# A two-norm, two-convolution kernel: another order of norms and results, and result c folded into its last product and copied by ScalarE

## Chip, cores and metric

The kernel runs on one core of one Trainium2 chip. The metric is the device time of one execution in microseconds. Shown are the median of several runs, and one profiled execution with its trace.

## The reference, cut to what matters

`x` is (16, 384, 32, 32) in fp32, `offset` is (48, 2). All arithmetic is fp32.

```python
x = x + _L0_conv_ref(_gn(x), L0_conv_offset)
x = x + _L1_conv_ref(_gn(x))
return x
```

`_gn` is a group norm with 32 groups of 12 channels per image. `_L0_conv_ref` shifts each block of 8 channels by its own whole number of pixels, zeroes what comes from outside, and applies one 3x3 Gaussian kernel per block, depthwise. Only a few of the 48 blocks have an offset that leaves anything in view. `_L1_conv_ref` multiplies the 384 channels of each pixel, padded to 512, by a Hadamard matrix over the square root of 512 and keeps the first 384 outputs.

## The kernel before

**Data and quarters.** The 16 images go in four quarters of four. A ring of ten places in SBUF holds whole images: 384 channels are three tiles a, b, c of 128 partitions, 1024 pixels each. SP loads them (L389), also stores the results from the same place (L421), and a place is loaded again once its three stores have landed.

**First norm and convolution.** For each quarter, statistics of every channel are taken, on ScalarE by two passes over a tile (`take_stats`, L559) and on VectorE by `bn_stats` (L1044); `dve_tiles` (L51) says which engine takes which tile. VectorE turns them into means (`means`, L1059), PE sums them over groups (`sum_means`, L687), VectorE spreads them (L1074), PE sums again (`sum_about`, L696), and `unit_moments`, ScalarE's `root_first` and `unit_scales` give the scale of each block. Nine blocks in view are computed in three units of a quarter: two of four blocks each ("strips"), and one of one block cut in four bands. SP fetches a unit's rows twice from DRAM, shifted and plain (`fetch`, L394). ScalarE norms the shifted rows (`centre`, L576), PE transposes them (`transposes`, L715), VectorE masks them (L1118), PE convolves (L746), and VectorE adds the plain rows and takes statistics of the sum (`add`, L1130). GpSimd then writes the sum x1 to DRAM (`leave`, L477) and gathers its rows back over the images in the ring with six indirect DMAs per quarter (`gather`, L496). Other channels have x1 = x and stay. `more_blocks` handles offsets with more blocks in view and does not run here.

**Second norm.** `all_moments`, `sum_second` (PE, L777), `second_shift`, ScalarE's `root_second` and `second_scale` give the scale of each channel and image, and `sum_bias` with `second_bias` the output bias.

**Products and results.** Per image n, PE accumulates into one pair of PSUM banks, `ps[n % 2]`. `product_a` (L798) multiplies tile a in fp32 by a scaled 128x128 Hadamard block; `product_b` subtracts tile b, given as two fp16 parts that ScalarE (`high`, L612) and VectorE (`low`, L1262) make; `product_c` adds tile c in fp32. That is the result for output tile b. VectorE's `result` (L1268) adds bias and x1 and writes it over the ring. Then `add_b` adds twice tile b: output tile a. Then `add_c` subtracts twice tile c: output tile c. Each waits for the result before it, since it overwrites the same banks, and `product_a` of image n waits for all three results of image n-2. The order is b, a, c. The weight of tile c lies in `w_c` in two versions, one scaled by h and one by -2h, made by ScalarE for the first image of a quarter (`weights_c`, L607) and by GpSimd for the others (L505).

**Order.** Every engine's order is written out by hand. The head does quarter 0 up to its products. Then window w (w = 0 to 3) holds the results of images 4w to 4w+3 and, among them, norm, units and second norm of quarter w+1 and the statistics of quarter w+2; `j` is the image's number in its quarter. SP's loop is at L459, GpSimd's at L544, ScalarE's at L643, PE's at L874, VectorE's follows its head. Three places matter below: VectorE does `means(q)` ahead of the first result of a window; it does all of mask, add and `all_moments` at j = 1 ahead of the first result of j = 2; and PE's second sums wait for these moments:

```python
if j == 1:
    ...
    if units:
        mask(g + 2)
        add(g + 1)
        add(g + 2)
        all_moments(q)
if j == 2:
    result(n, 1)
```

## Time and profile before

| | us |
|---|---|
| median of 3 runs (289.92 to 291.0) | 290.21 |
| profiled execution, its own time | 289.43 |
| its span in the trace | 287.6 |
| DVE busy | 178.9 |
| PE busy | 177.8 |
| ACT busy | 117.4 |
| POOL busy | 72.4 |

The span runs from the first to the last instruction of the profiled execution; 1.8 us of its time lie outside. PE is TensorE, DVE VectorE, ACT ScalarE, POOL GpSimd, SP the engine that issues most DMAs. A row of a timeline gives the start and the duration of an instruction or of several merged ones, and in brackets the idle time of its engine before it with what released it. L815 is the matmul of tile b, L825 that of tile c, L808 that of tile a, L1272 the result, L1265 the low part, L618 the high part, L565 and L568 ScalarE's two statistics passes.

### The profile page before, as it was taken

The numbers are of one execution on the slowest core, as the hardware profiler recorded it, in microseconds if no ns is written. First come the engines' busy times: TensorE is split into PE (matmuls) and PEld (weight loads), VectorE is DVE, ScalarE is ACT, GpSimd is POOL, SyncE is SP. The second block draws the span as 40 slices with busy tenths as digits, with TensorE's granted clock in tenths as the row PEclk, the third lists the DMA queues.
The fourth block names the chain that finished last, engine by engine and source line by source line (L and its number), as shares of the span: only waits on it lengthen the run. The fifth ranks groups of instructions, "written<-read, shape, count | busy, mean of one in ns | idle before, by whom it ended". The sixth has DMA issues, their size and how long they took to land.

```text
span 287.6 us, 3917 instructions
## 1 busy us (share of the span) xinstructions
PE 177.8 (62%) x1228; PEld 89.7 (31%) x1228; DVE 178.9 (62%) x411; ACT 117.4 (41%) x179; POOL 72.4 (25%) x101
## 2 busy tenths in 40 slices
PE   1300158306529776586597981957779839899962
PEld 1200046203204524242245351412345424233420
DVE  2779745921757585745976638448966476666642
ACT  0295088013937595098038780692231001311000
POOL 0197001328600000581200004742000036720000
PEclk9999999955969999599869997799799977999998
DMA  6999999915555176399899983896874325855544
GB/s 212 400 416 407 239 289 408 411 63 162 154 172 223 75 215 263 132 312 351 279 258 320 377 293 149 267 359 234 214 274 172 147 93 170 291 217 219 219 194 170
DMA packets 23626, 70.65 MB, mean 246 GB/s; under 512 B 5952, under 2 KB 6976, under 8 KB 23024
## 3 DMA queue, kind: packets, MB, share of 16 engines
q1 hardware_dynamic: 18480, 60.90, 60.4%
q0 software_dynamic: 5120, 9.45, 10.5%
q8 instruction: 11, 0.18, 0.2%
q14 instruction: 15, 0.12, 0.1%
HBM read 60.89 MB, written 29.88 MB: 316 GB/s over the span
## 4 chain that ended last, share of the span: by engine, by line
PE 39%; DVE 35%; ACT 10%; issue 8%; DMA 4%; POOL 1%; DVEq 0%; SPq 0%; POOLq 0%; ACTq 0%
PE ps L825 12%; DVE ring L1272 10%; PE ps L815 8%; PE ps L730 7%; PE ps L808 6%; DVE halves L1049 5%; ACT junk L565 4%; DVE unit_half L1140 4%; DVE plain L1137 4%; ACT junk L568 4%; PE ps L711 4%; DMA ring<-x_rows,index 2%; DVE flip L1109 2%; DMA x_rows<-plain 2%; DVE parts L1265 1%
## 5 line engine op out<-in xcount | busy, mean ns | idle before, releaser
L1272 DVE SCALAR_TENSOR_TENSOR ring<-ps,out_bias,ring 128x1024 f32<-128x1024 f32 x48 | 61.5, 1282 | 36.7 <-PE ps L825 20.3
L825 PE MATMUL ps<-ring,w_c 128*128 128x512 f32 x128 | 61.0, 615 | 5.7 <-DVE ring L1272 5.6
L815 PE MATMUL ps<-parts,had_sb 128*128 128x512 f16 x128 | 41.0, 463 | 13.8 <-DVE ring L1272 9.7
L618 ACT ACTIVATE parts<-ring,scale 128x1024 f16<-128x1024 f32 x16 | 18.0, 1143 | 62.7 <-PE ps L815 50.0
L808 PE MATMUL ps<-ring,w_a 128*128 128x512 f32 x64 | 32.0, 624 | 12.8 <-DMA ring<-x_rows,index 8.5
L565 ACT ACTIVATE junk<-ring 128x1024 f32<-128x1024 f32 x32 | 36.6, 1144 | 4.0 <-DMA ring<-x_pad 2.0
L481 POOL DMA_DIRECT2D x_rows<-plain x8 | 5.0, 620 | 128.7 <-DVE plain L1137 128.7
L568 ACT ACTIVATE junk<-ring 128x1024 f32<-128x1024 f32 x32 | 36.8, 1149 | 1.0
L825 PEld LDWEIGHTS ps<-ring,w_c 128*128 128x128 f32 x128 | 23.8, 197 | 35.2 <-issue 21.7
L1265 DVE SCALAR_TENSOR_TENSOR parts<-ring,scale,parts 128x1024 f16<-128x1024 f32 x16 | 20.6, 1288 | 18.9 <-ACT parts L618 18.9
L491 POOL DMA_INDIRECT ring<-x_rows,index x24 | 24.4, 1019 | 18.6 <-issue 18.6
L815 PEld LDWEIGHTS ps<-parts,had_sb 128*128 128x128 f16 x128 | 12.5, 112 | 37.5 <-DVE ring L1272 15.1
L730 PE MATMUL ps<-conv_w,flip 128*32 128x192 f32 (+2 forms) x640 | 23.4, 304 | 1.1 <-DVE plain L1137 1.1
L692 PE MATMUL ps<-means,sum_w 128*128 128x12 bf16 x28 | 1.3, 171 | 34.0 <-DVE means L1042 34.0
L808 PEld LDWEIGHTS ps<-ring,w_a 128*128 128x128 f32 x64 | 11.7, 198 | 28.8 <-issue 28.1
L1049 DVE BATCH_NORM_STATS2 halves<-ring 128x6 f32<-128x512 f32 x32 | 19.6, 673 | 1.4 <-issue 1.4
L730 PEld LDWEIGHTS ps<-conv_w,flip 128*32 128x32 f32 x640 | 17.9, 116 | 5.7 <-issue 2.6
L598 ACT ACTIVATE root<-var,geo_sb 128x12 f32<-128x12 f32 x4 | 1.2, 304 | 43.8 <-DVE var L1245 43.8
L1137 DVE TENSOR_TENSOR plain<-ps,plain 128x1024 f32<-128x1024 f32 (+1 forms) x12 | 11.3, 938 | 9.9 <-PE ps L730 9.9
L711 PE MATMUL ps<-geo_sb,shifted 128*128 128x128 f32 x72 | 11.8, 308 | 8.6 <-DVE flip L1109 5.9
L1109 DVE TENSOR_TENSOR flip<-ps,view 128x1024 f32<-128x1024 f32 x8 | 9.8, 1225 | 10.0 <-PE ps L711 9.8
L580 ACT ACTIVATE shifted<-shifted,unit_norm 128x1024 f32<-128x1024 f32 (+1 forms) x12 | 11.6, 1019 | 6.5 <-DMA shifted<-x_pad 3.7
(151 smaller groups left out, 168.6 us busy)
## 6 DMA issues: line engine op xcount, KB each, us to landing
ring<-x_pad SPq DMA_DIRECT2D x16, 1536.0 KB, 12.2
out<-ring SPq DMA_DIRECT2D x48, 512.0 KB, 3.4
shifted<-x_pad SPq DMA_DIRECT2D x32, 128.0 KB, 5.0
plain<-x_pad SPq DMA_DIRECT2D x32, 128.0 KB, 3.8
x_rows<-plain POOLq DMA_DIRECT2D x8, 512.0 KB, 4.8
shifted<-x_pad SPq DMA_DIRECT2D x16, 32.0 KB, 4.4
plain<-x_pad SPq DMA_DIRECT2D x16, 32.0 KB, 3.0
x_rows<-plain POOLq DMA_DIRECT2D x16, 32.0 KB, 1.7
```

The lines of the kernel that those rows point to most:

```text
L491: pool.indirect_dma_start(ring[:, t, first_place:first_place + 2, :].rearrange("p b n -> p (b n)"), None, x1_rows[q][0:BIND * slots, :].re ...
L565: act.activation(junk[:, :], image, ACT.Identity, bias=image[:, 0:1], scale=-1.0, accum_out=accum[:, q % 2, 0, t, b:b + 1]).then_inc(act_s ...
L568: act.activation(junk[:, :], image, ACT.Square, bias=image[:, 0:1], scale=-1.0, accum_out=accum[:, q % 2, 1, t, b:b + 1]).then_inc(act_sta ...
L711: last = pe.transpose(turned[:, j // 4, 128 * (j % 4):128 * (j % 4) + rows], shifted[0:rows, u, 128 * j:128 * (j + 1)], eye[0:rows, 0:rows])
L730: last = pe.matmul(summed[32 * s:32 * s + 32, bank, 32 * (lo - 16 * bank):32 * (hi - 16 * bank)], pixels[:, j, 32 * s:32 * s + 32], conv_w ...
L808: pe.matmul(ps[n % 2][:, h, :], w_a[:, n % 4, :], ring[:, 0, place_of(n), 512 * h:512 * (h + 1)], start=True, stop=False, skip_group_check ...
L815: last = pe.matmul(ps[n % 2][:, h, :], had_sb[:, 128 * sign:128 * (sign + 1)], parts[:, n % 2, part, s, 512 * h:512 * (h + 1)], start=Fals ...
L825: last = pe.matmul(ps[n % 2][:, h, :], w_c[:, n % 4, twice, :], ring[:, 2, place_of(n), 512 * h:512 * (h + 1)], start=False, stop=True, sk ...
L1049: last = dve.bn_stats(halves[:, q % 2, t, b, h, :], ring[:, t, place_of(i), 512 * h:512 * (h + 1)])
L1137: dve.tensor_tensor(plain[:, u, 0:width], sums, plain[:, u, 0:width], ALU.add).then_inc(x1_ready, 1)
L1265: dve.scalar_tensor_tensor(parts[:, n % 2, 1, s, :], ring[:, 1 + s, place_of(n), :], scale[:, q % 2, 1 + s, b:b + 1], parts[:, n % 2, 0, s ...
L1272: dve.scalar_tensor_tensor(ring[:, t, place_of(n), :], pixels_of(ps[n % 2]), out_bias[:, q % 2, t, b:b + 1], ring[:, t, place_of(n), :], A ...
```

## The change

Norm 1 is moved ahead of the results: VectorE's `means(1)`, `spread_means(1)`, `unit_moments(1)` and `unit_scales(1)`, PE's two sums and ScalarE's root now stand in the head, and the statistics of quarter 1 with them, split six tiles to six. SP fetches the shifted rows of two units of quarter 1 before it waits for the gathered rows, loads before it stores, and does the next window's wait and shifted fetch at j = 2. The results of a window are interleaved with masks and adds, the second sums stand ahead of the last image's additions, and all products of the next quarter's first image follow them. Result c loses its VectorE instruction: `fold_weights` builds -2h times the scale plus the identity per image, so that `add_c` adds x1 of tile c in the same matmuls, and ScalarE's `result_c` copies PSUM with the bias to the ring. `result_done` now counts two per image, `result_c_done` the third.

In the diff the orders of ScalarE, PE and VectorE are shown as they are after it, without the removed lines, which are in the code above.

```diff
 def dve_tiles(i):
     if i < 2 * QUARTER:
-        return ((0, 1), (0,))[i // QUARTER]
+        return (0, 1) if i < QUARTER + 2 else (0,)
     return (0, 1) if i % QUARTER == QUARTER - 1 else ()
...
-        w_c = sb("w_c", [128, 4, 2, 128])
+        w_c = sb("w_c", [128, 4, 128])
+        w_fold = sb("w_fold", [128, 2, QUARTER, 128])
...
-            def fetch(q):
+            def fetch(q, which, units=range(UNITS)):
                 def rows(tile, u, s, which):
                     if SLOTS_OF[u] == 1:
                         return tile[32 * s:32 * s + 32, u, 0:WIDTH_OF[u]], x_bands(q, at[PER_UNIT * u][which])[:, s, :]
                     return tile[32 * s:32 * s + 32, u, :], x_slot(q, at[PER_UNIT * u + s][which])
 
-                for u in range(UNITS):
-                    if q:
-                        sp.wait_ge(flipped, UNITS * (q - 1) + u + 1)
-                    for s in range(PER_UNIT):
-                        home, source = rows(shifted, u, s, 1)
-                        sp.dma_start(home, source).then_inc(shifted_in[u], 16)
-                for u in range(UNITS):
-                    if q:
+                for u in units:
+                    if which == 1:
+                        if q:
+                            sp.wait_ge(flipped, UNITS * (q - 1) + u + 1)
+                    elif q:
                         sp.wait_ge(x1_out[u], left(u, q - 1))
                         sp.wait_ge(x1_stat, UNITS * (q - 1) + u + 1)
                     for s in range(PER_UNIT):
-                        home, source = rows(plain, u, s, 0)
-                        sp.dma_start(home, source).then_inc(plain_in[u], 16)
+                        home, source = rows((plain, shifted)[which], u, s, which)
+                        sp.dma_start(home, source).then_inc((plain_in, shifted_in)[which][u], 16)
...
             def store(n, t):
-                sp.wait_ge(result_done, CT * n + ORDER.index(t) + 1)
+                if t == 2:
+                    sp.wait_ge(result_c_done, n + 1)
+                else:
+                    sp.wait_ge(result_done, 2 * n + ORDER.index(t) + 1)
                 sp.dma_start(out_v[n][:, t, :], ring[:, t, place_of(n), :]).then_inc(store_out[place_of(n)], 16)
...
-            fetch(0)
+            fetch(0, 1)
+            fetch(0, 0)
             for i in range(QUARTER + 2, RING):
                 sp.wait_ge(load_in[place_of(i - 4)], 16)
                 load(i)
             active = sp.value_load(count_i[0:1, 0:1], min_val=0, max_val=OFFSETS)
+            fetch(1, 1, (0, 1))
             more_blocks(0)
             rows_back(0)
-            fetch(1)
+            fetch(1, 1, (2,))
+            fetch(1, 0)
             for n in range(BATCH):
                 w, j = n // QUARTER, n % QUARTER
-                store(n, 1)
-                store(n, 0)
                 if n >= 1 and n - 1 + RING < BATCH:
                     load(n - 1 + RING)
-                store(n, 2)
+                for t in ORDER:
+                    store(n, t)
                 if j == 1 and w + 1 < QUARTERS:
                     more_blocks(w + 1)
+                if j == 2 and w + 2 < QUARTERS:
+                    rows_back(w + 1)
+                    fetch(w + 2, 1)
                 if j == 3 and w + 2 < QUARTERS:
-                    rows_back(w + 1)
-                    fetch(w + 2)
+                    fetch(w + 2, 0)
...
-                pool.tensor_scalar(w_c[:, n % 4, 0, :], geo_of("h"), scale[:, q % 2, 2, b:b + 1], None, ALU.mult)
-                pool.tensor_scalar(w_c[:, n % 4, 1, :], geo_of("h"), scale[:, q % 2, 2, b:b + 1], -2.0, ALU.mult, ALU.mult)
+                pool.tensor_scalar(w_c[:, n % 4, :], geo_of("h"), scale[:, q % 2, 2, b:b + 1], None, ALU.mult)
                 pool.tensor_scalar(w_a[:, n % 4, :], geo_of("h"), scale[:, q % 2, 0, b:b + 1], None, ALU.mult).then_inc(weights_ready, 1)
...
-                act.activation(w_c[:, n % 4, 0, :], geo_of("h"), ACT.Copy, scale=scale[:, q % 2, 2, 0:1])
-                act.activation(w_c[:, n % 4, 1, :], geo_of("minus_2h"), ACT.Copy, scale=scale[:, q % 2, 2, 0:1]).then_inc(first_weights_c, 1)
+                act.activation(w_c[:, n % 4, :], geo_of("h"), ACT.Copy, scale=scale[:, q % 2, 2, 0:1]).then_inc(first_weights_c, 1)
+
+            def result_c(n):
+
+
+                q, b = n // QUARTER, n % QUARTER
+                act.wait_ge(product_done, CT * n + CT)
+                act.activation(ring[:, 2, place_of(n), :], pixels_of(ps[n % 2]), ACT.Identity,
+                               bias=out_bias[:, q % 2, 2, b:b + 1]).then_inc(result_c_done, 1)
...
-            for i in range(QUARTER, QUARTER + 2):
+            for i in range(QUARTER, 2 * QUARTER):
                 for t in act_tiles(i):
                     take_stats(i, t)
             root_second(0)
             weights(0)
             weights_c(0)
-            for n in range(2):
-                high(n, 0)
-            for i in range(QUARTER + 2, 2 * QUARTER):
-                for t in act_tiles(i):
-                    take_stats(i, t)
-            for n in range(BATCH):
-                w, j = n // QUARTER, n % QUARTER
+            high(0, 0)
+            high(1, 0)
+            root_first(1)
...
+            for w in range(QUARTERS):
+                n, g = QUARTER * w, UNITS * (w + 1)
                 units, stats_next = w + 1 < QUARTERS, w + 2 < QUARTERS
                 ahead = QUARTER * (w + 2)
+                high(n + 2, 0)
+                result_c(n)
+                if units:
+                    if w:
                         root_first(w + 1)
+                    for u in range(UNITS):
+                        centre(g + u)
+                if stats_next:
+                    take_stats(ahead, 0)
+                high(n + 3, 0)
+                if stats_next:
+                    take_stats(ahead, 1)
+                result_c(n + 1)
+                if stats_next:
+                    take_stats(ahead, 2)
+                    take_stats(ahead + 1, 0)
+                result_c(n + 2)
+                if stats_next:
+                    take_stats(ahead + 1, 1)
+                if units:
+                    more_blocks(w + 1)
+                    root_second(w + 1)
+                    weights(n + QUARTER)
+                    weights_c(n + QUARTER)
+                if stats_next:
+                    take_stats(ahead + 1, 2)
+                result_c(n + 3)
+                if stats_next:
+                    take_stats(ahead + 2, 0)
+                if units:
+                    high(n + QUARTER, 0)
+                    high(n + QUARTER + 1, 0)
+                if stats_next:
+                    take_stats(ahead + 2, 1)
+                    take_stats(ahead + 2, 2)
+                    take_stats(ahead + 3, 2)
 
...
-                    pe.wait_ge(result_done, CT * (n - 1))
+                    pe.wait_ge(result_done, 2 * (n - 1))
+                    pe.wait_ge(result_c_done, n - 1)
...
+                weight = w_fold[:, q % 2, b, :] if twice else w_c[:, n % 4, :]
                 for h in range(2):
-                    last = pe.matmul(ps[n % 2][:, h, :], w_c[:, n % 4, twice, :], ring[:, 2, place_of(n), 512 * h:512 * (h + 1)],
+                    last = pe.matmul(ps[n % 2][:, h, :], weight, ring[:, 2, place_of(n), 512 * h:512 * (h + 1)],
                                      start=False, stop=True, skip_group_check=True)
...
-                pe.wait_ge(result_done, CT * n + 1)
+                pe.wait_ge(result_done, 2 * n + 1)
                 product(n, 0, B_TWICE, True).then_inc(product_done, 1)
 
             def add_c(n):
-                pe.wait_ge(result_done, CT * n + 2)
+                pe.wait_ge(result_done, 2 * n + 2)
+                pe.wait_ge(fold_ready, n // QUARTER + 1)
                 tile_c(n, 1).then_inc(product_done, 1)
...
             sum_second(0)
+            sum_means(1)
             product_a(0)
+            sum_about(1)
             sum_bias(0)
             product_b(0)
             product_c(0)
             product_a(1)
...
+            for w in range(QUARTERS):
+                n, g = QUARTER * w, UNITS * (w + 1)
+                units = w + 1 < QUARTERS
+                add_b(n)
+                product_b(n + 1)
+                if units and w:
+                    sum_means(w + 1)
+                add_c(n)
+                if units and w:
+                    sum_about(w + 1)
+                product_c(n + 1)
+                product_a(n + 2)
+                if units:
+                    transposes(g)
+                add_b(n + 1)
+                product_b(n + 2)
+                if units:
+                    transposes(g + 1)
+                    convolve(g)
+                add_c(n + 1)
+                product_c(n + 2)
+                if units:
+                    transposes(g + 2)
+                    convolve(g + 1)
+                product_a(n + 3)
+                add_b(n + 2)
+                product_b(n + 3)
+                if units:
+                    convolve(g + 2)
+                add_c(n + 2)
+                product_c(n + 3)
+                if units:
+                    more_blocks(w + 1)
+                    sum_second(w + 1)
+                add_b(n + 3)
+                if units:
+                    sum_bias(w + 1)
+                add_c(n + 3)
+                if units:
+                    product_a(n + 4)
+                    product_b(n + 4)
+                    product_c(n + 4)
+                    product_a(n + 5)
...
-                if q >= 2:
-                    link(mean_and_variance(QUARTER * q + QUARTER - 1, stats_at[QUARTER * q + QUARTER - 1]))
+                if q:
+                    for i in range(QUARTER * q, QUARTER * q + QUARTER):
+                        if dve_tiles(i):
+                            last = mean_and_variance(i, stats_at[i])
+                    link(last)
...
+            def fold_weights(q):
+                for b in range(QUARTER):
+                    last = dve.scalar_tensor_tensor(w_fold[:, q % 2, b, :], geo_of("minus_2h"), scale[:, q % 2, 2, b:b + 1], geo_of("eye"),
+                                                    ALU.mult, ALU.add)
+                last.then_inc(fold_ready, 1)
...
             mask(0)
+            take_stats(4, (0,))
             mask(1)
+            stats_at[4] = take_stats(4, (1,))
+            take_stats(5, (0,))
             add(0)
             mask(2)
-            stats_at[4] = take_stats(4)
+            stats_at[5] = take_stats(5, (1,))
             add(1)
-            mean_and_variance(4, stats_at[4])
             add(2)
             all_moments(0)
             second_shift(0)
             second_scale(0)
+            fold_weights(0)
+            stats_at[6] = take_stats(6)
+            stats_at[7] = take_stats(7)
+            means(1)
+            spread_means(1)
             low(0, 0)
+            unit_moments(1)
+            low(1, 0)
             bias_at[0] = second_bias(0)
-            low(1, 0)
-            for i in range(QUARTER + 1, 2 * QUARTER):
-                stats_at[i] = take_stats(i)
-                if i > QUARTER + 1:
-                    mean_and_variance(i - 1, stats_at[i - 1])
-            link(mean_and_variance(2 * QUARTER - 1, stats_at[2 * QUARTER - 1]))
-            for n in range(BATCH):
-                w, j = n // QUARTER, n % QUARTER
-                q = w + 1
-                units, stats_next, g = q < QUARTERS, w + 2 < QUARTERS, UNITS * (w + 1)
+            unit_scales(1)
...
+            for w in range(QUARTERS):
+                n, g, q = QUARTER * w, UNITS * (w + 1), w + 1
+                units, stats_next = q < QUARTERS, w + 2 < QUARTERS
                 ahead = QUARTER * (w + 2)
+                result(n, 1)
+                if units and w:
+                    means(q)
+                result(n, 0)
+                if units and w:
+                    spread_means(q)
+                if units and w:
+                    unit_moments(q)
+                low(n + 2, 0)
+                if units and w:
+                    unit_scales(q)
+                result(n + 1, 1)
+                if units:
+                    keep_moments(q)
+                    mask(g)
+                result(n + 1, 0)
+                if units:
+                    mask(g + 1)
+                    add(g)
+                low(n + 3, 0)
+                if units:
+                    mask(g + 2)
+                result(n + 2, 1)
+                if units:
+                    add(g + 1)
+                result(n + 2, 0)
+                if units:
+                    add(g + 2)
+                    all_moments(q)
+                if units:
+                    second_shift(q)
+                result(n + 3, 1)
+                if units:
+                    second_scale(q)
+                result(n + 3, 0)
+                if units:
+                    bias_at[q] = second_bias(q)
+                    fold_weights(q)
+                if stats_next:
+                    stats_at[ahead + 3] = take_stats(ahead + 3)
+                if units:
+                    low(n + 4, 0)
+                    low(n + 5, 0)
```

## Rows read from the trace of the kernel before

**Rows 1.** The page: busy time of each engine; GB/s moved in 40 equal slices

```profile
PE 177.8 (62%) x1228; PEld 89.7 (31%) x1228; DVE 178.9 (62%) x411; ACT 117.4 (41%) x179; POOL 72.4 (25%) x101
...
GB/s 212 400 416 407 239 289 408 411 63 162 154 172 223 75 215 263 132 312 351 279 258 320 377 293 149 267 359 234 214 274 172 147 93 170 291 217 219 219 194 170
```

**Rows 2.** Stretches: length, busy of PE, PEld, DVE, ACT, POOL, then clock, DMA share, GB/s

```profile
83.30:141.90 58.60, 42.65 (x304) 20.69 (x304) 38.67 (x83) 33.32 (x52) 13.92 (x21) 0.91 0.65 224
141.90:202.20 60.30, 44.38 (x304) 21.60 (x304) 38.69 (x84) 33.43 (x52) 13.94 (x21) 0.89 0.86 284
202.20:254.50 52.30, 40.93 (x301) 20.65 (x302) 34.92 (x68) 9.05 (x12) 14.89 (x21) 0.90 0.58 193
254.50:287.60 33.10, 24.42 (x68) 9.40 (x66) 17.93 (x14) 2.30 (x2) 0.00 (x0) 0.97 0.51 206
```

**Rows 3.** Waits: engine, line, releaser: us in total, times, longest

```profile
PE ps L692 <- DVE means L1042: 34.0, 4, 22.3
...
PE ps L782 <- DVE scrap L942: 20.4, 4, 5.4
```

**Rows 4.** Timeline of DVE: start us, us, operation, [idle before it, releaser]

```profile
81.87 0.17 DVE L1062 TENSOR_SCALAR deviation<-accum 128x8 f32<-128x8 f32 x1 [4.61 <-ACT junk L568]
...
101.60 1.21 DVE L1137 TENSOR_TENSOR plain<-ps,plain 128x1024 f32<-128x1024 f32 x1
...
104.29 1.23 DVE L1265 SCALAR_TENSOR_TENSOR parts<-ring,scale,parts 128x1024 f16<-128x1024 f32 x1
...
114.46 0.38 DVE L1137 TENSOR_TENSOR plain<-ps,plain 128x256 f32<-128x256 f32 x1
...
117.57 1.28 DVE L1272 SCALAR_TENSOR_TENSOR ring<-ps,out_bias,ring 128x1024 f32<-128x1024 f32 x1
```

**Rows 5.** Timeline of PE, head and window 0

```profile
67.20 3.58 PE L808 MATMUL ps<-ring,w_a 128*128 128x512 f32 x4 [8.50 <-DMA ring<-x_rows,index]
...
72.56 1.88 PE L825 MATMUL ps<-ring,w_c 128*128 128x512 f32 x4
...
84.65 1.89 PE L815 MATMUL ps<-parts,had_sb 128*128 128x512 f16 x4 [0.77 <-DVE ring L1272]
...
93.17 1.04 PE L711 MATMUL ps<-geo_sb,shifted 128*128 128x128 f32 x8
...
96.67 2.72 PE L730 MATMUL ps<-conv_w,flip 128*32 128x160 f32 x80
...
99.32 1.90 PE L815 MATMUL ps<-parts,had_sb 128*128 128x512 f16 x8
...
101.74 3.70 PE L825 MATMUL ps<-ring,w_c 128*128 128x512 f32 x8 [0.52 <-DVE ring L1272]
...
111.62 1.18 PE L739 MATMUL ps<-conv_w,band_flip 128*128 128x160 f32 x8
...
118.91 3.25 PE L815 MATMUL ps<-parts,had_sb 128*128 128x512 f16 x8 [0.62 <-DVE ring L1272]
```

**Rows 6.** Timeline of ACT

```profile
39.45 1.15 ACT L565 ACTIVATE junk<-ring 128x1024 f32<-128x1024 f32 x1 [0.19 <-issue]
...
42.05 1.15 ACT L565 ACTIVATE junk<-ring 128x1024 f32<-128x1024 f32 x1
...
59.61 0.30 ACT L598 ACTIVATE root<-var,geo_sb 128x12 f32<-128x12 f32 x1 [9.82 <-DVE var L1245]
...
89.78 2.87 ACT L580 ACTIVATE shifted<-shifted,unit_norm 128x1024 f32<-128x1024 f32 x3 [1.18 <-DVE unit_norm L1103]
```

**Rows 7.** Timeline of POOL; then DMA issues at 49.1 and 136.3, to landing

```profile
62.69 1.10 POOL L491 DMA_INDIRECT ring<-x_rows,index  x1 [5.51 <-issue]
...
119.49 1.10 POOL L491 DMA_INDIRECT ring<-x_rows,index  x1 [2.35 <-issue]
...
x_rows<-plain POOLq DMA_DIRECT2D x1, 512.0 KB, 8.4
...
ring<-x_pad SPq DMA_DIRECT2D x1, 1536.0 KB, 10.5
```

138 lines of the change are left out of this document (5 added, 133 removed).

## The prediction

> **What bounds the kernel now.** I began with the page: the busiest engine, DVE, works 62% of the span and PE 62% [rows 1]. So no engine is full, and the time lies in how the engines wait for each other. The table by stretches [rows 2] is cut at the starts of the first result of batches 0, 4, 8 and 12. It leaves a head of 83.3 us before its first row, and gives three windows of 58.6, 60.3 and 52.3 us (four batches of results, the unit work of the next quarter beside them) and a tail of 33.1 us. In each window PE is busy 41 to 44 us and DVE 35 to 39 us; the tail has PE 24.4 of 33.1. The granted clock is 0.89 to 0.91 of full in the windows.
>
> The waits by releaser [rows 3] name the two holes on PE: 34.0 us before the sums of the means and 20.4 us in four waits of about 5 us before the second sums (L782). In the DVE timeline [rows 4] the head's hole is plain: DVE sits idle for 4.61 us at 81.87 for ScalarE's statistics, then computes the means, and only then takes result b of batch 0 at 83.3, though PE had that product from 74.4 on (the fp32 matmuls at 72.56 last 1.88) [rows 5]. Result b of batch 2 starts at 117.57 because VectorE's order puts it behind all the adds and moments; PE had finished it at about 105.4 (101.74 + 3.70) [rows 5]. So the order written by hand binds, not the amount of work.
>
> **The change, part by part.** Prices of one piece, at the full clock: four fp16 matmuls 0.87 (eight take 1.90), four fp32 ones 1.72, the eight transposes 1.0, a strip convolution 2.7, the band one 1.18 [rows 5]; on DVE a result or a low part 1.20 to the next start, an add with its statistics 2.7 (101.60 to 104.29) [rows 4]; on ACT a tile of statistics 2.6 (39.45 to 42.05), a high part, one pass over the same 128x1024, 1.15, the three centrings 2.87 [rows 6].
>
> *The head.* Norm 1 moves ahead of the results. ScalarE's share of its statistics goes from 8 tiles to 6, all before the second root: 6 x 2.6 = 15.6 from 39.45 ends at 55.1; the root came at 59.61 [rows 6], so this is hidden, with 4.5 to spare for loads that land late. VectorE takes 6 tiles at 1.2 instead of 4; four fit into its waits for transposes and convolutions, two (2.5 us), the four fold instructions (below) and the means (about 2.7 with the aggregates) stand between 60.7 and 67. Product a of batch 0 waits for its gathered rows until 67.20 [rows 5], so they are hidden too, with a few tenths to spare; bound: 0 to 1.5. The first result then starts when product c ends, 74.4, not 83.3: minus 8.9. Against this, SP now fetches the shifted rows of two units of quarter 1 (8 x 128 KB, 1 MB) at 40 to 45 us, behind the last ring loads. Beside those the x1 write of the first unit takes 8.4 us to land [rows 7], and the gather waits for all the x1 writes. At the 410 GB/s of that stretch [rows 1] 1 MB is 2.6 us: between 0 (the fetch only queues behind its own) and 2.6 I take 1.5. The page DMA: Bandwidth & Descriptors of the Trainium skill (Queues, rings and completion order) says each DMA engine goes round-robin between queues, packet by packet. By that rule the fetch would not stand ahead of the writes but only keep their share low for longer, which is inside the same bounds. **Start of the results: 74.4 + 1.5 = 75.9.**
>
> *ScalarE takes result c.* DVE loses 16 of 48 results (19 us at 1.20), ACT gets 16 copies out of PSUM. No row shows ACT reading PSUM; the nearest are the high part (1.15) and a centring of 1024 columns, an Identity with bias too, whose three take 2.87 with one of a quarter's size, so about 1.25: I take 1.15, and up to 1.3. The page VectorE: DVE Perf Modes (The TRN2 errata) gives a ScalarE copy from PSUM fewer fixed cycles than one from SBUF; its figures would make it about 1.0 us, an estimate, and the sum would be the same, since these copies end before product a of the next-but-one batch asks for them. What they cost is the place in ACT's queue, counted below. PE's work is equal: the identity is folded into a weight it loads anyway. The fold is four DVE instructions on 128x128 per quarter; bounds 0.17 (a vector of 128x8) and 0.38 (the band add, 128x256) each [rows 4], I take 0.9 for the four, behind PE's last product c, so nothing on the path. POOL and ACT lose one weight scaling each.
>
> *Window 0.* From the first result, PE's own order now has hardly a hole: product a 1.7; b twice 1.75 and a 0.5 wait for result a; c twice 3.5; a 1.7 (9.2); transposes (10.2); b twice (11.9); transposes and strips (15.6); c twice (19.05); band transposes, strips (22.1); a (23.8); b twice (25.55); bands (26.75); c twice (30.2); second sums (30.8). Masks, adds and results of DVE fit beside it: the first add ends at 18.4, before the second strips end; the second add's 2.7 and result a of batch 2 end at 26.1, before 26.75. Moments end at 29.9. What used to be 5 us before L782 is gone. Then comes the part bound by turns: second shift 0.9 and result b 1.25 (33.0), b again and its result a (35.3), c again (37.0). ACT then has result c (38.2), one tile of statistics (40.8) and the high part (42.0); DVE low part (43.3); half of product b and product c: **45.5**. The x1 round trip is near but not last: from the band add (114.46 [rows 4]) to the first gather (119.49) are 5.0, and 4.5 more to its landing (62.69 to 67.20, [rows 5, 7]), for which I take 5.2 beside stores, 1.4 later for tile b: 27.2 + 5.0 + 1.4 + 5.2 = 38.8.
>
> *Window 1.* Ten tiles (26 us) of statistics, four copies, four high parts and three centrings fill ACT for about 39 us. Behind the high parts (43.1) three tiles are still queued: 7.8, to 50.9, 5.4 into window 1. VectorE's means of that window wait for them and sit ahead of result a, so c again starts at 8.6 instead of 4.0, and with the sums the transposes end at 15.1, not 10.2: plus 4.9, **50.4**. This is a new wait, and the same one moves on into window 2, where no statistics follow: there the gather ends last: 32.1 + 5.0 + 1.4 + 5.2 = 43.7, then 1.15 + 1.25 + 0.45 + 1.75: **48.3**.
>
> SP: the wait for the gathered rows and 12 fetches of the next window now precede the stores of batch n+3 and load 12. Issued near 51 in window 0, landing 10.5 later as at 136.3 [rows 7], it comes at 61.5, just when ScalarE wants it (15.6 into window 1). Zero, at most 2 per window.
>
> *The clock.* After a hole PE runs at half speed for a while: four fp16 matmuls took 1.89 at 84.65 and eight 3.25 at 118.91, against 0.87 and 1.90 [rows 5], together 2.4 us a window. The holes are shorter in window 0 (about 4 us while the high part is made) and a real 4 us returns with the means: 1.5, 2.4 and 2.4.
>
> *The tail* keeps its order on PE; its last result is now ACT's, 1.15 for 1.28: 33.1.
>
> **Sum.** 75.9 + 47.0 + 52.8 + 50.7 + 33.1 = 259.5 against a span of 287.6. Around the span lay 1.8 (289.43 profiled): 261.3. The median of the runs is 0.8 above that execution: **262**.
>
> **The rivals.**
> *ScalarE's queue and the loads bind more than I say.* For it: ACT waits in strict order for a product, a load, a root and a product again, and load 12 has no slack. Each of windows 0 to 2 is 3 to 4 longer: 262 + 10 = 272. Chance 0.17.
> *Only the head gains.* If the windows keep their 58.6, 60.3 and 52.3 because the x1 round trip and the half clock hold them, the time is 290.2 - 7.4 (83.3 - 75.9) = 283. Against it: result b of batch 2 alone waited 12 us for nothing. Chance 0.08.
> *The copies do not help.* If an ACT copy out of PSUM took 2 us or more, the tail's product a would wait, since product a follows result c after only one more fp32 product, 1.72: 0.5 x 12 batches, some 6 us: 268. Chance 0.05.
> *Slower.* One mechanism: SP stands at the gathered rows while the ring places of stored batches wait for reloading; loads 12 to 15 arrive late, ACT's statistics wait in front of its copies, and so PE's product a. It decides once load 12 lands about 14 us later than needed in each of two windows, that is once the sum loses its 28. The landing of 10.5 us [rows 7] speaks against this. Chance 0.05: 0.04 for 293, 0.01 that it stops at no change.
> *Better than forecast.* The clock stays full and the fetch costs nothing: 256. Chance 0.12.
>
> **How the numbers follow.** The forecast itself has 0.53, with its own range of 258 to 267 (DMA 0 to 2.6, hidden head work 0 to 1.5, clock 0 to 7). The range 255 to 275 takes in the better case, the slow copy and the ScalarE rival, leaving out 283 and the slower one. A difference of 0.5% is about what a measurement of this kernel can tell from none. Faster 0.95, same 0.01, slower 0.04.
>
> **What would show it.** Right: first result at 75 to 77; PE's waits for means far below 34 us and for the second sums under 1 each; in windows 1 and 2 a DVE wait of 3 to 5 for ACT before the means; result c copies of 1.0 to 1.3; window lengths near 47, 53 and 51. Wrong: a gather that starts after 66; a product a released by an ACT copy; ACT idle for ring loads.

## The result, and the profile after

The changed kernel takes **267.25 us** (median of 4 runs, 266.63 to 267.69) against 290.16 (4 runs) for the kernel before: a ratio of **0.9204**, 95% interval 0.9174 to 0.9234. The forecast was 262, its range 255 to 275. The profiled execution took 266.63, with a span of 264.6, for which the sum said 259.5. A second set of runs, later and on another chip, gave 268.07 (0.9244, 0.9175 to 0.9313). All ratios leave out single executions that came out 1.5% or more above the fastest of their kernel, while the medians take in all, and two of the profiles below, of no prefetch and of light and stats, are of such an execution, 4.4 and 3.1 us above the median.

The page of the changed kernel, busy time of each engine and four groups of lines (busy and mean ns, then idle time before them):

```profile
PE 178.2 (67%) x1228; PEld 93.7 (35%) x1228; DVE 166.8 (63%) x417; ACT 127.3 (48%) x183; POOL 68.7 (26%) x89
...
L1298 DVE SCALAR_TENSOR_TENSOR ring<-ps,out_bias,ring 128x1024 f32<-128x1024 f32 x32 | 41.0, 1282 | 27.7 <-PE ps L841 18.3
L622 ACT ACTIVATE ring<-ps,out_bias 128x1024 f32<-128x1024 f32 x16 | 17.8, 1113 | 68.7 <-PE ps L841 68.7
...
L631 ACT ACTIVATE parts<-ring,scale 128x1024 f16<-128x1024 f32 x16 | 17.9, 1141 | 28.7 <-PE ps L830 14.9
```

PE works as long as before (178.2 for 177.8); what went is its waiting. VectorE has 32 results for 48 and ScalarE the other 16, at 1113 ns each. The stretches, cut where they were cut before (first result of batches 0, 4, 8, 12), and then three pieces of windows 0 and 1:

```profile
75.28:123.66 48.38, 41.83 (x289) 21.53 (x288) 31.59 (x59) 31.86 (x47) 13.97 (x19) 0.89 0.71 239
123.66:184.52 60.86, 46.75 (x305) 23.52 (x304) 35.03 (x82) 39.35 (x60) 13.91 (x20) 0.83 0.84 286
184.52:231.65 47.13, 41.74 (x305) 22.11 (x304) 32.76 (x78) 14.88 (x19) 13.55 (x18) 0.93 0.79 267
231.65:264.60 32.95, 24.41 (x68) 9.53 (x66) 12.80 (x10) 6.75 (x6) 0.00 (x0) 0.97 0.47 191
...
75.30:105.50 30.20, 29.68 (x261) 16.27 (x260) 21.47 (x37) 18.65 (x25) 3.95 (x8) 1.00 0.75 250
...
139.50:161.00 21.50, 21.38 (x239) 12.82 (x237) 16.18 (x31) 15.10 (x24) 3.19 (x6) 1.00 0.92 308
161.00:184.40 23.40, 13.62 (x27) 5.76 (x28) 9.86 (x21) 15.31 (x25) 9.63 (x12) 0.71 0.74 272
```

Against [rows 2]: the head lost 8.0 us, window 0 10.2 and window 2 5.2. **Window 1 lost nothing** (60.9 for 60.3). It holds a stretch of 21.5 us in which PE does not stop at all, at full clock, and behind it 23.4 us with PE busy for 13.6 at a mean clock of 0.71. So its time went into the last part of the window, where PE waits.

The waits of the changed kernel, then those of SP's queue:

```profile
ACT ring L622 <- PE ps L841: 68.7, 16, 9.8
...
PE ps L706 <- DVE means L1057: 34.0, 4, 22.2
...
DVE halves L1064 <- DMA ring<-x_pad: 9.1, 1, 9.1
...
PE ps L796 <- DVE scrap L957: 5.3, 1, 5.3
```

```profile
SPq L395 <- DMA out<-ring: 37.9, 5, 12.4
```

The second sums have one wait of 5.3 left of four [rows 3]. The 34.0 before the sums of the means look unchanged, but 22.2 of them are the start of the kernel, as were 22.3 before; a later row shows the window's share. New are VectorE's 9.1 for a ring load, and 37.9 (4.0 in the kernel before) in which a load stood at stores that had not landed.

The timeline of PE and of DVE and ACT at the start of window 1:

```profile
125.17 1.89 PE L830 MATMUL ps<-parts,had_sb 128*128 128x512 f16 x8
130.51 0.34 PE L706 MATMUL ps<-means,sum_w 128*128 128x12 bf16 x7 [3.45 <-DVE means L1057]
131.62 2.07 PE L841 MATMUL ps<-ring,w_fold 128*128 128x512 f32 x2 [0.77 <-DVE ring L1298]
```

```profile
127.23 1.15 ACT L574 ACTIVATE junk<-ring 128x1024 f32<-128x1024 f32 x1
...
128.38 1.13 ACT L631 ACTIVATE parts<-ring,scale 128x1024 f16<-128x1024 f32 x1
```

```profile
128.51 0.17 DVE L1077 TENSOR_SCALAR deviation<-accum 128x12 f32<-128x12 f32 x1 [3.57 <-ACT junk L574]
```

This is the forecast's new wait: ScalarE ends its three queued tiles of statistics 4.7 us into the window (said: 5.4), the sums of the means stand idle for 3.45, and c again begins at 131.62, 8.0 into the window (said: 8.6; 4.0 in the order without the wait).

The later part of windows 0 and 1 on POOL (first the last x1 writes, then the first gather), and SP's loads around them:

```profile
103.37 1.48 POOL L491 DMA_DIRECT2D x_rows<-plain  x3 [0.30 <-issue]
112.10 1.09 POOL L498 DMA_INDIRECT ring<-x_rows,index  x1 [7.25 <-issue]
...
157.57 2.00 POOL L491 DMA_DIRECT2D x_rows<-plain  x4 [3.16 <-DVE plain L1155]
166.39 1.09 POOL L498 DMA_INDIRECT ring<-x_rows,index  x1 [6.82 <-issue]
```

```profile
102.74 0.40 SPq L395 DMA_DIRECT2D ring<-x_pad  x1
...
154.82 0.40 SPq L395 DMA_DIRECT2D ring<-x_pad  x1
```

In the kernel before, the gather of window 0 was issued at 119.49 after an idle 2.35 [rows 7] and SP's load only behind it:

```profile
122.58 0.43 SPq L392 DMA_DIRECT2D ring<-x_pad  x1
```

How long the four small x1 writes of window 0 took to land, from the DMA issues of that stretch, first after, then before:

```profile
x_rows<-plain POOLq DMA_DIRECT2D x4, 32.0 KB, 6.0
```

```profile
x_rows<-plain POOLq DMA_DIRECT2D x4, 32.0 KB, 1.7
```

Earlier results free the ring's places earlier, and SP's new order puts the load ahead of an image's stores. The 1.5 MB load (1536 KB), which used to follow the first gather, and the stores now start 0.6 us ahead of the last three of the four small x1 writes (the first is issued at 102.54), and these four take 6.0 us instead of 1.7. The gather, which waits for them, comes 10.3 us after the band add (101.83 in the DVE timeline), not 5.0. In window 1 it is 9.5 (156.86 to 166.39), and load 15 is issued just behind it, at 167.61.

### The profile page after: what moved, and what is told of

Read it like the earlier page. It is cut to its first block, busy times and chain, and to the rows that moved or that the text cites. A ratio compares the mean times of both kernels' runs of the same rounds, so it can differ in the third digit from the quotient of the medians.

```text
span 264.6 us, 3915 instructions
## 1 busy us (share of the span) xinstructions
PE 178.2 (67%) x1228; PEld 93.7 (35%) x1228; DVE 166.8 (63%) x417; ACT 127.3 (48%) x183; POOL 68.7 (26%) x89
## 4 chain that ended last, share of the span: by engine, by line
PE 46%; DVE 21%; DMA 14%; issue 8%; ACT 8%; POOL 2%; DVEq 0%; POOLq 0%; SPq 0%; ACTq 0%
PE ps L841 18%; PE ps L823 8%; DMA x_rows<-plain 7%; PE ps L830 7%; PE ps L744 6%; DMA ring<-x_rows,index 5%; DVE halves L1064 5%; DVE ring L1298 5%; PE ps L725 4%; ACT junk L571 3%; ACT junk L574 2%; POOL x_rows L491 2%; ACT parts L631 1%; DVE plain L1155 1%; PE ps L753 1%
## 5 line engine op out<-in xcount | busy, mean ns | idle before, releaser
L1298 DVE SCALAR_TENSOR_TENSOR ring<-ps,out_bias,ring 128x1024 f32<-128x1024 f32 x32 | 41.0, 1282 | 27.7 <-PE ps L841 18.3
L622 ACT ACTIVATE ring<-ps,out_bias 128x1024 f32<-128x1024 f32 x16 | 17.8, 1113 | 68.7 <-PE ps L841 68.7
L830 PE MATMUL ps<-parts,had_sb 128*128 128x512 f16 x128 | 33.6, 399 | 16.7 <-DVE ring L1298 8.4
L841 PE MATMUL ps<-ring,w_fold 128*128 128x512 f32 x64 | 38.6, 733 | 6.1 <-DVE ring L1298 6.1
L823 PE MATMUL ps<-ring,w_a 128*128 128x512 f32 x64 | 33.8, 654 | 6.0 <-issue 3.3
L571 ACT ACTIVATE junk<-ring 128x1024 f32<-128x1024 f32 x30 | 34.3, 1142 | 4.0 <-DMA ring<-x_pad 2.7
L574 ACT ACTIVATE junk<-ring 128x1024 f32<-128x1024 f32 x30 | 34.5, 1149 | 1.0
L841 PE MATMUL ps<-ring,w_c 128*128 128x512 f32 x64 | 32.4, 630 | 0.0
L631 ACT ACTIVATE parts<-ring,scale 128x1024 f16<-128x1024 f32 x16 | 17.9, 1141 | 28.7 <-PE ps L830 14.9
L1064 DVE BATCH_NORM_STATS2 halves<-ring 128x6 f32<-128x512 f32 x36 | 22.1, 675 | 10.5 <-DMA ring<-x_pad 9.1
L841 PEld LDWEIGHTS ps<-ring,w_fold 128*128 128x128 f32 x64 | 12.8, 223 | 19.6 <-issue 10.6
L841 PEld LDWEIGHTS ps<-ring,w_c 128*128 128x128 f32 x64 | 12.8, 203 | 14.1 <-issue 13.5
```

Of the source, the lines that this page charges most:

```text
L571: act.activation(junk[:, :], image, ACT.Identity, bias=image[:, 0:1], scale=-1.0, accum_out=accum[:, q % 2, 0, t, b:b + 1]).then_inc(act_s ...
L574: act.activation(junk[:, :], image, ACT.Square, bias=image[:, 0:1], scale=-1.0, accum_out=accum[:, q % 2, 1, t, b:b + 1]).then_inc(act_sta ...
L631: act.activation(parts[:, n % 2, 0, s, :], ring[:, 1 + s, place_of(n), :], ACT.Copy, scale=scale[:, q % 2, 1 + s, b:b + 1]).then_inc(high_ ...
L823: pe.matmul(ps[n % 2][:, h, :], w_a[:, n % 4, :], ring[:, 0, place_of(n), 512 * h:512 * (h + 1)], start=True, stop=False, skip_group_check ...
L830: last = pe.matmul(ps[n % 2][:, h, :], had_sb[:, 128 * sign:128 * (sign + 1)], parts[:, n % 2, part, s, 512 * h:512 * (h + 1)], start=Fals ...
L841: last = pe.matmul(ps[n % 2][:, h, :], weight, ring[:, 2, place_of(n), 512 * h:512 * (h + 1)], start=False, stop=True, skip_group_check=True)
```

## The experiments

A stretch is named head, windows 0, 1 and 2, tail, all cut as above. Behind the first measurement the kernels ran in three groups, each beside the kernel before: order only, fold only, light loads and stats last (beside 289.75); stats to DVE, loads held, held and stats and no prefetch (289.44); the others (289.42). Columns of the table are us of the profiled span's parts, then the median and its ratio.

| kernel | head | w0 | w1 | w2 | tail | median | ratio (95%) |
|---|---|---|---|---|---|---|---|
| before | 83.3 | 58.6 | 60.3 | 52.3 | 33.1 | 290.16 | 1 |
| changed | 75.3 | 48.4 | 60.9 | 47.1 | 33.0 | 267.25 | 0.9204 (0.9174 to 0.9234) |
| changed, again | 77.2 | 49.3 | 59.7 | 46.4 | 32.9 | 268.07 | 0.9244 (0.9175 to 0.9313) |
| order only | 75.7 | 48.1 | 60.6 | 52.6 | 34.9 | 271.74 | 0.9365 (0.9326 to 0.9405) |
| fold only | 81.4 | 62.2 | 63.1 | 51.0 | 32.9 | 292.74 | 1.0099 (1.0065 to 1.0133) |
| light loads | 77.6 | 47.9 | 54.8 | 51.9 | 33.0 | 267.83 | 0.9255 (0.9211 to 0.93) |
| stats last | 75.4 | 48.6 | 60.4 | 48.0 | 33.0 | 269.84 | 0.9323 (0.9281 to 0.9365) |
| stats to DVE | 77.7 | 49.5 | 55.3 | 47.1 | 32.9 | 265.01 | 0.9169 (0.9125 to 0.9213) |
| loads held | 78.7 | 52.6 | 59.2 | 47.1 | 33.0 | 272.48 | 0.9407 (0.9359 to 0.9455) |
| held and stats | 75.9 | 51.8 | 60.0 | 47.5 | 32.9 | 271.26 | 0.9388 (0.933 to 0.9445) |
| no prefetch | 73.7 | 49.5 | 59.8 | 51.8 | 34.4 | 266.78 | 0.9174 (0.9123 to 0.9224) |
| light and stats | 78.0 | 49.1 | 50.6 | 46.7 | 34.6 | 257.78 | 0.8894 (0.8844 to 0.8944) |
| stats, no prefetch | 74.2 | 50.7 | 55.0 | 47.6 | 33.0 | 262.59 | 0.9105 (0.9043 to 0.9168) |
| stats, stores first | 75.4 | 52.1 | 55.8 | 46.3 | 34.6 | 266.66 | 0.9221 (0.9166 to 0.9276) |

The tails of 34.4 to 34.9 have a mean clock of 0.93 to 0.94, the others 0.97 or more: the last fp32 products of the order-only kernel took 3.68 for 1.98.

**The two halves of the change.** Order only: the changed kernel with result c of all four batches back on VectorE and the second weights as before.

```diff
-                result_c(n)
...
+                result(n, 2)
...
-                weight = w_fold[:, q % 2, b, :] if twice else w_c[:, n % 4, :]
-                    last = pe.matmul(ps[n % 2][:, h, :], weight, ring[:, 2, place_of(n), 512 * h:512 * (h + 1)],
+                    last = pe.matmul(ps[n % 2][:, h, :], w_c[:, n % 4, twice, :], ring[:, 2, place_of(n), 512 * h:512 * (h + 1)],
```

> The new order alone: result c is VectorE's again, with the plain weights; ScalarE copies nothing. Theory (the order carries the gain, the copy on ScalarE little): 267 to 271 us. Rival (the relief of VectorE is what lets the order work: VectorE was 63% busy and sits on the path through masks and adds): 275 us or more, with PE losing its full stretch of 30 us after the first result.

Fold only: the kernel before, its order of norm and results kept, with the fold and ScalarE's copy.

```diff
+                    result_c(n)
...
-                result(n, 2)
...
                         bias_at[q] = second_bias(q)
+                        fold_weights(q)
```

> The old order with result c folded and copied by ScalarE. Theory (order binds): 287 to 291 us, since result b of image 2 still waits behind the adds and the means still stand before the first result. Rival (the 1.2 us per result on VectorE counts): 280 us or less.

The order alone takes 18 us (289.75 to 271.74, 0.7 above the range expected), the fold alone costs 3 (292.74, above its range of 287 to 291). In the fold-only kernel the four waits before the second sums are all there:

```profile
PE ps L710 <- DVE means L1063: 30.2, 4, 22.3
...
PE ps L800 <- DVE scrap L963: 20.4, 4, 5.4
```

So relieving an engine gains nothing while the order of its queue is what PE waits for; what the 3 us are isn't shown. On top of the new order the fold is worth 4.5 us here (271.74 to 267.25; 3.7 to the later runs), and the intervals don't touch: the one of the order alone begins at 0.9326, those of the changed kernel end at 0.9234 and 0.9313. In the profiles 5.5 us lie in window 2, where PE waits 3.55 for the means and takes 3.50 for c again without the fold, 0.67 and 1.98 with it. But two other kernels that have the fold show the long wait too and 51.8 and 51.9 for that window, and the profile of the order alone is of the longest of its four executions. So which part of the kernel the 4.5 come from isn't settled.

**Does the DMA traffic lengthen window 1?** Light loads: loads 14 and 15 bring 64 of 1024 pixels.

```diff
+                kept_pixels = 64 if i >= 14 else PIXELS
-                sp.dma_start(ring[:, :, place_of(i), :], x_batch(i)).then_inc(load_in[place_of(i)], 16)
+                sp.dma_start(ring[:, :, place_of(i), 0:kept_pixels], x_batch(i)[:, :, 0:kept_pixels]).then_inc(load_in[place_of(i)], 16)
```

> The changed kernel, but the loads of images 14 and 15 bring 64 of 1024 pixels of each channel, so the statistics and results of these two images are computed on what lay there; all instructions and waits stay. Theory (window 1 took 60.8 us instead of 52.8 because loads 14 and 15 stand in the DMA queues beside the x1 writes and the gather, and VectorE waits for load 15): window 1 falls to 51 to 54 us, the gather starts under 6 us after the band add instead of 9, 259 us in all. Rival (the window is long because of the half clock and ScalarE's queue): window 1 stays above 58, 265 to 267 us.

Window 1 fell by 6.1, to 54.8 (51 to 54 was expected), and window 2 rose by 4.8, so the time didn't fall at all, where 259 was expected. Nor did the gather come under 6 us after the band add: it came at 7.1 (158.51 to 165.63) for 9.5. The high part of tile b then starts 49.9 into the window for 53.1, and PE, idle for 2.20 ahead of it and not 5.09, runs product c behind it at full clock, 1.88 for 3.53. The stretches, and PE at the start of window 2:

```profile
125.42:180.19 54.77, 44.28 (x305) 22.79 (x304) 35.05 (x82) 36.61 (x56) 14.59 (x21) 0.88 0.83 276
180.19:232.11 51.92, 43.98 (x305) 23.15 (x304) 32.97 (x78) 17.51 (x23) 13.54 (x18) 0.87 0.67 231
```

```profile
187.13 0.33 PE L707 MATMUL ps<-means,sum_w 128*128 128x12 bf16 x7 [3.53 <-DVE means L1058]
188.24 3.78 PE L842 MATMUL ps<-ring,w_fold 128*128 128x512 f32 x4 [0.77 <-DVE ring L1299]
```

The wait for the means is back (3.53), and the fp32 products behind it run at half clock (3.78 for four; four at full clock take 1.98 in the tail of the changed kernel). In the changed kernel this wait is 0.67 in window 2: its slow end of window 1 gave ScalarE the time to work off its tiles. **The two causes**, the ring loads and ScalarE's backlog, **hide each other**, and making these two loads light brings nothing alone.

**Is it ScalarE's queue?** Stats last: VectorE takes its own share of the last statistics behind the two low parts, not ahead of them.

```diff
-                    stats_at[ahead + 3] = take_stats(ahead + 3)
...
+                    stats_at[ahead + 3] = take_stats(ahead + 3)
```

> The changed kernel with VectorE's statistics of image 4w+11 behind the two low parts instead of ahead of them. If VectorE's own wait of 9.1 us for load 15 is what holds window 1, it falls by 5 us or more, to 261 us. Theory (the high part waits for the gather until 176.75 anyway, and the low part would start at 177.9 instead of 178.8): minus 1 us, 266 us.

No stretch moved by 1 us, and the median is 269.84 against the changed kernel's 267.25 and 268.07 (the profiled execution, 267.39, is the fastest of the four): no gain, where 266 was expected. In this kernel the order of VectorE's own statistics is not the cause.

Stats to DVE: two more tiles of each window go from ScalarE to VectorE.

```diff
-    return (0, 1) if i % QUARTER == QUARTER - 1 else ()
+    return (0, 1) if i % QUARTER >= QUARTER - 2 else ()
```

with ScalarE's one tile of that batch ahead of its high parts, and VectorE's two ahead of its low parts. VectorE's statistics of the last image go behind the low parts, as in stats last; all later variants except no prefetch have that too.

> The changed kernel with VectorE taking tiles a and b of image 4w+10 too, so ScalarE has 8 tiles a window instead of 10, one of them left behind the high parts instead of three. Theory (two bounds in turn: in window 1 the late DMAs, in window 2 ScalarE's backlog before the means as soon as the DMAs are on time): window 0 unchanged at 48, window 1 loses the 5 us wait for the means but keeps the late gather, so it gets 3 to 5 us shorter; 261 to 264 us. Rival (only the DMAs bind): 267 us.

Its window 1 and its waits before the means:

```profile
127.23:182.55 55.32, 45.40 (x308) 22.71 (x307) 37.53 (x89) 31.73 (x47) 12.95 (x18) 0.90 0.92 314
```

```profile
PE ps L704 <- DVE means L1055: 29.9, 2, 22.3
```

Two waits of the four are gone (34.0 to 29.9), window 1 is 5.5 shorter, and the clock in it 0.90 for 0.83. The median moved 2 to 3 us, since head and window 0 were longer in this profile (77.7 and 49.5); at 265.01 it is 1 above the range expected, and its interval overlaps those of the changed kernel.

Window 1 did not keep its late gather, though. Without the wait for the means the band add is at 154.70, 27.5 into the window for 33.2, and the x1 writes go out before load 14 (155.41 against 157.44). The four small ones land in 2.0 us, the gather comes 5.1 after the band add, and the high part starts 43.8 into the window for 53.1. All of this with the full loads. PE has ended product c by 175.9, but VectorE takes the first result of window 2 only at 182.55, since its statistics of image 15 stand ahead of it and wait for load 15:

```profile
180.16 2.47 DVE L1062 BATCH_NORM_STATS2 halves<-ring 128x6 f32<-128x512 f32 x4 [5.48 <-DMA ring<-x_pad]
```

So once ScalarE's backlog is gone, what is left of the DMA traffic in window 1 is this wait, and not the x1 round trip.

**Can the traffic be put off?** Loads held: the stores go first, and the loads of images 11 and 15 stand behind the wait for the gathered rows.

```diff
-                if n >= 1 and n - 1 + RING < BATCH:
-                    load(n - 1 + RING)
...
+                if j != 1 and n + RING < BATCH:
+                    if j == 2:
+                        rows_back(w + 1)
+                        load(n - 1 + RING)
+                    load(n + RING)
...
-                    rows_back(w + 1)
+                    if w:
+                        rows_back(w + 1)
+                        load(n - 1 + RING)
```

> The changed kernel with SP storing before loading, and with the loads of images 11 and 15 held until the gathered rows of the next quarter are back, so that no ring load stands beside x1 writes or a gather; VectorE's statistics of image 4w+11 behind the low parts. Theory: from the band add to the first gather 5.0 us again in windows 0 and 1; window 0 46, window 1 54, window 2 52 with ScalarE's backlog back: about 265 us. Rival (DMAs alone bind): window 1 51, window 2 47, 258 us or less. If images 11 and 15 come too late for the means, window 0 or 1 grows by the difference.

> Both edits: held loads and ScalarE with 8 tiles. Theory (two bounds in turn): each alone gives 2 to 5 us, both together 10 us or more: windows of 46, 49 and 47, 254 to 258 us. Rival (one of the two is the cause): no better than the better of the two alone.

Both are slower than the changed kernel, 272.48 and 271.26, with window 0 at 52.6 and 51.8. My idea was wrong, though in window 0 the gather did come 5.9 and 6.2 us after the band add, not 10.3: there the held load comes too late, and VectorE waits for it ahead of the first result of window 1, by 3.69 and 3.31 (at window 1's end by 6.53 and 6.4). That is the last case that the expectation named. SP's queue around window 1 of the first:

```profile
141.55 0.40 SPq L395 DMA_DIRECT2D ring<-x_pad  x1
142.23 6.31 SPq L412 DMA_DIRECT2D plain<-x_pad  x12
148.59 2.37 SPq L426 DMA_DIRECT2D out<-ring  x3
157.75 0.40 SPq L395 DMA_DIRECT2D ring<-x_pad  x1
```

Loads 11 and 12 had gone out together at 122.16. Load 13 (141.55) follows with 12 fetches in front of the stores, and load 14 waits until 157.75. It stands beside the x1 writes of that window (153.89 to 164.29), and the gather comes 9.3 us after the band add, for 9.5 in the changed kernel: the traffic is not gone, it meets the next x1 writes.

Stats, stores first: the simpler form of it, with the stats edit.

```diff
-                if n >= 1 and n - 1 + RING < BATCH:
-                    load(n - 1 + RING)
...
+                if n + RING < BATCH:
+                    load(n + RING)
-                if j == 2 and w + 2 < QUARTERS:
+                if j == 3 and w + 2 < QUARTERS:
```

> ScalarE with 8 tiles, and SP issues the three stores of an image and then the load into the same place, with the gathered rows and both fetches of the window after next behind the stores of the fourth image. Theory (in the changed kernel each load waits for stores that stand behind the load before it in the same queue, so the loads of window 1 come 13 us apart, the last beside the gather): loads 12 to 15 land earlier, window 1 gets 2 to 4 us shorter, 261 us. Rival (the traffic of window 1 is the same in any order): 265 us or more.

266.66, no better than the 265.01 of the stats edit alone, where 261 was hoped for. So neither of the two other orders of SP's queue, held loads and stores first, helped.

**The fetch of the shifted rows in the head.** No prefetch: SP fetches them behind the head, as before.

```diff
-            fetch(1, 1, (0, 1))
-            fetch(1, 1, (2,))
+            fetch(1, 1)
```

> The changed kernel without the early fetch of quarter 1's shifted rows: all of it behind the gathered rows. Theory (the 1 MB keeps the x1 writes of the head from landing): the small x1 writes land in 3.5 us instead of 6.2 and the gather starts 2 us earlier in the head; the centring of quarter 1 then waits for its rows by 2 us or less, since they land near 78 and are asked for at 82. So 265 to 266.5 us. Rival (the prefetch is free): 267 to 269 us.

The first gather on POOL, without the fetch and with it:

```profile
54.76 1.99 POOL L490 DMA_DIRECT2D x_rows<-plain  x4 [1.26 <-DVE plain L1154]
61.92 1.10 POOL L497 DMA_INDIRECT ring<-x_rows,index  x1 [5.17 <-issue]
```

```profile
53.89 2.00 POOL L491 DMA_DIRECT2D x_rows<-plain  x4 [1.26 <-DVE plain L1155]
63.52 1.10 POOL L498 DMA_INDIRECT ring<-x_rows,index  x1 [7.64 <-issue]
```

From the last writes to the gather are 7.2 us without it, 9.6 with it: the fetch costs 2.5 us there. The start of the results moved from 75.3 to 73.7. The time, 266.78, is 0.3 above the range expected and can't be told from the changed kernel's.

**The changed kernel again**, to see how it varies:

> The changed kernel as it is, beside the variants on one chip: 267 us, windows of 48, 61 and 47 us.

Its head was 1.9 longer and its windows 1 and 2 shorter by 1.1 and 0.7: that much differs between executions of one program.

**Both causes at once.** Light and stats: the stats edit, and all loads from image 10 on light (`if i >= 10`).

> ScalarE with 8 tiles, and every ring load from image 10 on brings only 64 of 1024 pixels of each channel (images 10 to 15 are computed on what lay there). Theory (two bounds in series: DMA traffic in windows 0 and 1, ScalarE's backlog in the windows behind): with both gone windows of 46, 49 and 47 us, first gather 4 to 5 us after the band add in every window, 252 to 256 us. Rival (something else holds the windows, such as the half clock after the high part): window 1 stays at 54 or more and the time above 260.

Its three windows, and its POOL in window 0:

```profile
77.98:127.06 49.08, 42.40 (x291) 22.30 (x290) 33.76 (x63) 31.44 (x46) 12.82 (x18) 0.93 0.57 194
127.06:177.64 50.58, 43.31 (x303) 22.29 (x302) 37.52 (x89) 31.74 (x47) 14.28 (x18) 0.88 0.68 225
177.64:224.32 46.68, 42.49 (x305) 22.20 (x305) 32.99 (x80) 12.98 (x15) 13.53 (x18) 0.91 0.72 252
```

```profile
106.07 1.48 POOL L492 DMA_DIRECT2D x_rows<-plain  x3 [0.30 <-issue]
110.87 1.09 POOL L499 DMA_INDIRECT ring<-x_rows,index  x1 [3.32 <-issue]
```

257.78, 1.8 above the range expected: 7.2 below the stats edit, 10.1 below the light loads, where each alone had given 2 to 3 and nothing. Window 1 is at 50.6 and window 2 stays at 46.7. Two bounds stand one behind the other, ScalarE's backlog and the ring loads. The comparison isn't quite clean: here loads 10 to 15 are light, in the light loads only 14 and 15, and all six without the stats edit were not run.

Against the stats edit, the light loads don't shorten the x1 round trip of window 1: the gather comes 7.7 us after the band add (154.50 to 162.22), there 5.1. The high part starts at the same place of the window (43.6 for 43.8). What is gone is VectorE's wait of 5.48 for load 15. Window 0 hardly moved, though its gather comes 6.3 us after the band add (104.52 in its DVE timeline), not 10.3: there the turns between ScalarE, VectorE and PE end last, and the high part (121.11) follows ScalarE's statistics without a wait.

**The best that keeps all data.** Stats, no prefetch: the two edits together.

> ScalarE with 8 tiles and no early fetch of quarter 1's shifted rows. If both small gains add (2 us each over the changed kernel): 263 us, the best of all. If the head's gain is lost again because the centring or the adds wait for rows: 265.

262.59, ratio 0.9105 (0.9043 to 0.9168): below the kernel before and below the first measurement of the changed kernel (0.9174 to 0.9234). Beside the changed kernel of its own group (0.9175 to 0.9313) the intervals just don't touch.

## Why the prediction was right, and where its sizes were off

The direction, the mechanism and the range held: the hand-written order was the bound, and PE's idle time, span less busy, fell from 109.8 to 86.4 us. The likeliest time was 5 us low, and 267.25 lies just above the forecast case's own 258 to 267. Its steps, against the span:

| step | said | measured | difference |
|---|---|---|---|
| start of the results | 75.9 | 75.3 | -0.6 |
| window 0 | 47.0 | 48.4 | +1.4 |
| window 1 | 52.8 | 60.9 | +8.1 |
| window 2 | 50.7 | 47.1 | -3.6 |
| tail | 33.1 | 33.0 | -0.1 |

That the whole is only 5 off is in part luck: window 1 alone is 8.1 off, and 3.6 came back in window 2 for a reason that the forecast didn't have.

**The head** was right. The first result follows product c as said, the hidden norm work costs nothing, and the DMA term of 1.5 lies in its bounds, with the cost of 2.5 at the gather that the no-prefetch run shows partly covered by earlier x1 writes (53.89 here for 55.17 before). Executions of the same head end between 75.3 and 78.7, so more can't be read from it.

**ScalarE's copy** was priced at 1.15, measured at 1.11, and no product a is released by one. By the Trainium skill's page VectorE: DVE Perf Modes (The TRN2 errata) it would have been about 1.0, an estimate. The trace has 1.11 for the duration and 1.01 from a copy's start to that of the next instruction (103.63 to 104.64). It agrees that the read from PSUM is the cheaper one (1113 ns against 1141 for the high part, which differs in its output type too); by the page's cycles it would be 43 ns, an estimate.

**PE's order in window 0** was worked out piece by piece as hole-free for 30.8 us; the row shows 29.68 busy of 30.20 and the full clock.

**The wait for the means** is where it was said, with 8.0 for 8.6 at c again. One sign was badly chosen: PE's waits for the means were to fall far below 34 us, and are 34.0. The prediction had read the whole 34.0 as a hole of PE's, but 22.3 of them are the kernel's start, and of the rest 7.6 now lie in the head, where PE has nothing else to do. The one wait of 5.3 before the second sums is in the head too.

**The step that failed** is the x1 round trip, the 5.0 from band add to gather and the 5.2 to landing, together with "Zero, at most 2 per window" for SP. In window 1, counted from its start:

| point | said | measured |
|---|---|---|
| band add | 32.1 | 33.2 (156.86) |
| first gather | 37.1 | 42.7 (166.39) |
| high part of tile b | 43.7 | 53.1 (176.75) |

The band add is 1.1 late, the way to the gather 4.5 longer and the way to the high part 3.8 longer: 9.4 in all, and the window is 8.1 longer. I had taken the durations from places of the trace before where the loads came behind the gather. The forecast had the turns end last in that window, at 50.4, and the gather's way at 48.3; it was the gather's way. PE, idle for 5.09 ahead of product b, then ran product c at half clock, 3.53 for 1.88. The forecast counted what SP's queue waits for, but not what the faster engines make it issue sooner: a load and stores ahead of the x1 writes. The light loads show it from the other side, and so does the stats edit, whose x1 writes go out ahead of load 14: 5.1 from band add to gather. In window 0 the gather is 4.6 late too (36.8 into the window for 27.2 + 5.0), and the high part of tile b starts at 43.4 (118.67), not 38.8. But there the turns end about as late: ScalarE is through with its tile at 42.5 (117.78), for 40.8 said, since c again ran at half clock (110.45 on, 3.78 for 1.98), and idles only 0.89 before the high part.

The page DMA: Bandwidth & Descriptors (Queues, rings and completion order) of the Trainium skill says that a DMA engine takes the queues in turn, packet by packet. The trace agrees only in part: 32 KB writes on POOL's queue land in 6.0 us beside a load and stores on SP's queue, in 2.3 beside stores and a light load, in 1.7 in the kernel before; in window 0 they land between 108.5 and 110.3, estimates from their issues and these 6.0, and the load at 111.1 (102.74 and its 8.4). So they aren't put behind the whole 1.5 MB, but come hardly earlier than it.

**Window 2** was priced 3.6 too high. The waits for the means that were carried on to it need a ScalarE backlog at its start, and the late end of window 1 had removed it (0.67 for 3.45). With light loads it is there again, and window 2 takes 51.9, for the 50.7 said.

**The rivals.** The one named "ScalarE's queue and the loads bind more" was right in kind (removing both is worth 10 us, removing one 0 to 3), and its price of 3 to 4 in each window was wrong in place: nearly all of it lay in window 1. Only the head gains, copies that don't help, and slower are out. In the better case the fetch costs nothing and the clock stays full; the clock was 0.83 in window 1.

**Still open.** Window 0 stays at 49.1 with light loads where the turns alone would give 45.5 by my sum. Of these 3.6 about 2.5 are the half clock by its rows (b again 1.76 for 1.04, c again 3.78 for 1.98), where I had taken 1.5. How the DMA time divides between the ring load, the stores and the fetches was only half tried: with light loads the gather of window 1 still comes 7.1 and 7.7 us after the band add, so the loads are a part of the 4.5 and the rest wasn't taken apart. Where the fold's 4.5 us lie isn't shown. And with the stats edit VectorE's statistics of the last image, which wait 5.5 us for their load, could stand behind the first result of the next window; that order wasn't run.

## What to carry to other kernels

Where an engine with a hand-written order waits, the order is worth more than the load: moving work off an engine that isn't the bound brought nothing here, and even cost 3 us, until the order was mended. When a change makes results earlier, redraw the DMA queue with the new times before a landing time is taken from the old trace: every transfer that those results release moves forward too, and may now stand beside a short write that something waits for. And test two suspected bounds together as well as singly; here the single tests gave 0 and 2 to 3 us, the double one 10. Then read in each trace which wait ends last: the bound that the double test removed was another wait for the same loads than the one that I had named.
